# A map of row numbers that moves from a table of its own into the rows of x

## The reference

```python
x = layernorm(x + L0(x))     # two GIN convolutions and a linear layer
x = layernorm(x + L1(x))     # relational GCN, 8 edge types
x = layernorm(x + L2(x))     # GCN on the first 10000 nodes
x = layernorm(x + L3(x))     # three GAT layers

def gin_conv(x):             # in L0
    agg = segment_sum(x[src], dst, num_segments=50000)
    h = x + agg
    return relu(h @ wa + ba) @ wb + bb
```

## Time and profile before

| | |
|---|---|
| median of two runs | 3564.31 us (3557.01 to 3571.61) |
| span of the profiled execution | 5308.1 us |
| busy PE / DVE / ACT / POOL in it | 3134.5 / 2677.8 / 2356.1 / 2154.2 us |
| DMA packets, data | 430539, 673.46 MB |
| start block; dense part; gin1 | 0 to 49; 51 to 1465; 1465 to 1901 us |
| all other phases | 1901 to 5308 us |

### The profile page before, as it was taken

The page is one execution under the profiler, slowest core; times in us unless marked ns, Lnnn a source line. Parts: engine busy times, 40 slices in busy tenths (PEclk is TensorE's granted clock), DMA queues, the critical chain, the costliest instruction groups (busy, mean ns, idle before and its releaser), DMA issues. The chain is left out here.

```text
span 5308.1 us, 70155 instructions
## 1 busy us (share of the span) xinstructions
PE 3134.5 (59%) x18625; PEld 2527.0 (48%) x18625; DVE 2677.8 (50%) x8976; ACT 2356.1 (44%) x6177; POOL 2154.2 (41%) x2226
## 2 busy tenths in 40 slices
PE   1110107999867779868756403997029970178864
PEld 1000006777644445534446403996029870177764
DVE  1000008999943346559846301775006860199875
ACT  0000007999812224447735302775017750188765
POOL 6777760000045555546366473001740017500366
PEclk7555559999967777779967656987559975598555
DMA  2200004444434433425556423765227752276542
GB/s 77 56 9 8 18 9 140 174 172 170 164 117 127 119 87 108 112 90 168 164 155 200 142 63 104 225 196 163 62 72 233 220 177 61 58 245 232 169 125 82
DMA packets 430539, 673.46 MB, mean 127 GB/s; under 512 B 81411, under 2 KB 168086, under 8 KB 430252
## 3 DMA queue, kind: packets, MB, share of 16 engines
q1 hardware_dynamic: 354764, 558.83, 32.6%
q0 software_dynamic: 70464, 108.96, 8.9%
q10 hardware_dynamic: 5024, 2.30, 0.2%
HBM read 378.46 MB, written 295.50 MB: 127 GB/s over the span
## 5 line engine op out<-in xcount | busy, mean ns | idle before, releaser
L647 POOL DMA_INDIRECT msgs<-t_gat,row_i x600 | 574.3, 957 | 1081.6 <-POOLq L157 895.1
L664 POOL DMA_INDIRECT dg_g_ring<-in_x,dst_i x200 | 192.2, 961 | 860.5 <-DVE g_xb L1222 782.9
L2229 ACT ACTIVATE t_nnt<-t_p_nt,cxt 128x512 f32<-128x512 f32 x294 | 200.4, 682 | 756.0 <-remote 265.3
L1754 PE MATMUL t_p_q<-mean_col,t_nsq 128*128 128x1 f32 x2352 | 332.6, 263 | 273.2 <-issue 243.0
L1754 PEld LDWEIGHTS t_p_q<-mean_col,t_nsq 128*128 128x128 f32 x2352 | 342.9, 224 | 280.8 <-issue 280.8
L2023 POOL DMA_INDIRECT out_rows<-t_x,own_i x200 | 204.4, 1022 | 491.1 <-ACT t_x L2279 437.9
L2109 PE MATMUL t_p_nt<-ident,t_nh 128*128 128x128 f32 x1176 | 217.7, 316 | 309.3 <-issue 176.1
L1747 PE MATMUL t_p_nh<-wx,t_nnt 128*128 128x132 f32 x1568 | 265.1, 320 | 178.9 <-issue 156.1
L800 PE MATMUL de_p_o<-wc,de_hh 128*128 128x128 f32 x1568 | 225.8, 289 | 151.5 <-DVE de_r L948 124.3
L2109 PEld LDWEIGHTS t_p_nt<-ident,t_nh 128*128 128x128 f32 x1176 | 158.1, 163 | 328.9 <-issue 231.4
L1747 PEld LDWEIGHTS t_p_nh<-wx,t_nnt 128*128 128x128 f32 x1568 | 228.4, 221 | 179.9 <-issue 179.4
(11 more groups left out here) (405 smaller groups left out, 9434.7 us busy)
## 6 DMA issues: line engine op xcount, KB each, us to landing
t_nh<-t_gat SPq DMA_DIRECT2D x294, 264.0 KB
t_gat<-t_nhn SPq DMA_DIRECT2D x196, 264.0 KB
t_x<-de_x SPq DMA_DIRECT2D x196, 256.0 KB
t_ah<-t_gat SPq DMA_DIRECT2D x150, 264.0 KB
t_x<-t_x SPq DMA_DIRECT2D x148, 256.0 KB
t_gat<-t_ahn SPq DMA_DIRECT2D x100, 264.0 KB
t_gat<-de_h SPq DMA_DIRECT2D x98, 264.0 KB
de_x<-in_x SPq DMA_DIRECT2D x97, 256.0 KB
```

The source lines that it names most:

```text
L647: self.nc.gpsimd.indirect_dma_start(out=self.msgs[:, c, 0:width], out_offset=None, in_=table, in_offset=bass.IndirectOffsetOnAxis(ap=idx[: ...
L664: nc.gpsimd.indirect_dma_start(out=ring[:, u, j, :], out_offset=None, in_=a["x"], in_offset=bass.IndirectOffsetOnAxis(ap=self.dst_i[:, i * ...
L1754: last = self.nc.tensor.matmul(p_q[:, j:j + 1], sq[:, j * D:(j + 1) * D], self.mean_col[:], start=True, stop=True)
L2229: nc.scalar.activation(nnt[:, g % 2], p_nt[:], ACT.Identity, bias=bias).then_inc(act_nt, 1)
```

## The change

The map gets a place in the rows of x. A new table `t_xw` has rows of 129 floats: 128 of x and the row number as the 129th float. One indirect gather by `src` then brings x and the row number.

- The start block: ACT writes SLOTS + node into the 129th float of all 50176 rows, in seven DMAs of 4-byte elements, behind its loads. SP writes zeros into x's place in the rows N to NPAD, and the store of the old map goes. The `dst` list is loaded and turned first in place of `src`.
- The dense block: SP issues 16 DMAs that copy x, memory to memory, 3125 rows of 512 bytes each into rows 516 bytes apart, ahead of its first load of x.
- POOL: gathers x by `dst` into `msgs` (24 in the start block, 168 then, 8 later), waits for `map_filled` and scatters the slot numbers to every 129th float, waits for the copy and the scatters, and gathers rows of 129 floats by `src` into the ring. The 200 look-ups and the zeros into `msgs` go.
- gin1: `msgs` and the ring change places. DVE copies the 129th floats to `row_i` in every group, and ACT waits for DVE's sum of bias and `msgs` (`dve_b`) before it writes `hidden` over that part of `msgs`.
- Slots without an edge of their own (partition 0) gather the zero row N.

```diff
+MW = D + 1
+COPIES = 16
+FILLS = 7
+LATE = 8
...
-        self.where = dram("t_where", NPAD + SLOTS, 1, I32)
+        xw = nc.dram_tensor("t_xw", (NPAD * MW + SLOTS,), F32, kind="Internal").ap()
+        self.places = xw.rearrange("(r o) -> r o", o=1)
+        self.xw = xw[0:NPAD * MW].rearrange("(r w) -> r w", w=MW)
+        self.unplaced = xw[NPAD * MW:NPAD * MW + SLOTS].rearrange("(p c) -> p c", p=128)
...
                     act.dma_start(dst, src).then_inc(loaded, 16)
+                act.wait_ge(self.nodes_told, 1)
+                t = NPAD // 128
+                rows = self.xw[0:NPAD, D:MW].rearrange("(p t) o -> p (t o)", p=128)
+                for n in range(FILLS):
+                    part = slice(n * t // FILLS, (n + 1) * t // FILLS)
+                    act.dma_start(rows[:, part], self.node_row[:, part]).then_inc(self.map_filled, 16)
...
             sp.dma_start(self.t4[SLOTS:SLOTS + 128, :], spread[:, 3, :]).then_inc(stored, 16)
+            for n in range(N, NPAD, 128):
+                m = min(NPAD, n + 128)
+                sp.dma_start(self.xw[n:m, 0:D], spread[0:m - n, 3, :]).then_inc(stored, 16)
...
-    def slot_gathers(self, pool, ring, sem, arrived, turned, copied):
+    def slot_gathers(self, pool, ring, sem, arrived, turned, taken):
...
             for j in range(G4):
                 nc.gpsimd.indirect_dma_start(
-                    out=ring[:, u, j, :], out_offset=None, in_=a["x"],
-                    in_offset=bass.IndirectOffsetOnAxis(ap=self.dst_i[:, i * G4 + j:i * G4 + j + 1], axis=0)).then_inc(arrived[u], 16)
-
-        def look(c):
-            nc.gpsimd.indirect_dma_start(
-                out=self.row_i[:, c:c + 1], out_offset=None, in_=self.where,
-                in_offset=bass.IndirectOffsetOnAxis(ap=self.src_i[:, c:c + 1], axis=0)).then_inc(self.map_taken, 16)
-
-        self.resident_gather(self.src_i, a["x"], D, got, range(FIRST, CHUNKS))
+                    out=ring[:, u, j, :], out_offset=None, in_=self.xw,
+                    in_offset=bass.IndirectOffsetOnAxis(ap=self.src_i[:, i * G4 + j:i * G4 + j + 1], axis=0)).then_inc(arrived[u], 16)
+
+        self.resident_gather(self.dst_i, a["x"], D, self.got, range(FIRST, CHUNKS - LATE))
+        pool.wait_ge(self.map_filled, 16 * FILLS)
         for c in range(CHUNKS):
             nc.gpsimd.indirect_dma_start(
-                out=self.where, out_offset=bass.IndirectOffsetOnAxis(ap=self.put_i[:, c:c + 1], axis=0),
+                out=self.places, out_offset=bass.IndirectOffsetOnAxis(ap=self.put_i[:, c:c + 1], axis=0),
                 in_=self.slot_id[:, c:c + 1], in_offset=None).then_inc(mapped, 16)
-        for i in range(UN):
-            rows(i)
...
-        ahead = CHUNKS - (AG - UN)
-        for c in range(ahead):
-            look(c)
-        for i in range(UN, AG):
-            rows(i)
-            look(ahead + i - UN)
-        pool.wait_ge(self.map_taken, 16 * CHUNKS)
+        self.resident_gather(self.dst_i, a["x"], D, self.got, range(CHUNKS - LATE, CHUNKS))
+        pool.wait_ge(self.x_copied, 16 * COPIES)
+        pool.wait_ge(mapped, 16 * CHUNKS)
+        for i in range(AG):
+            rows(i)
...
                 sp.wait_ge(s["cleared"], 1)
+                for n in range(COPIES):
+                    part = slice(n * N // COPIES, (n + 1) * N // COPIES)
+                    sp.dma_start(self.xw[part, 0:D], a["x"][part, :]).then_inc(self.x_copied, 16)
...
                     if live(k, u, 4, AG):
                         act.wait_ge(s["pe_b"], i - 3)
+                        act.wait_ge(s["dve_b"], i - 3)
...
+                    if live(k, u, 1, AG):
+                        dve.wait_ge(arrived[v], 16 * G4 * (k + (0 if u < 1 else 1)))
+                        nc.vector.tensor_copy(self.row_i[:, bass.ds((i - 1) * G4, G4)], xs[:, v, :, D]).then_inc(s["dve_row"], 1)
```

More of the change, by code:

```diff
@@ L178, in allocate @@
         self.got = ctx.enter_context(nc.semaphore("got"))
+        self.x_copied = ctx.enter_context(nc.semaphore("x_copied"))
+        self.map_filled = ctx.enter_context(nc.semaphore("map_filled"))
         def sb(name, shape, dt=F32):
@@ L416, in turn @@
             last.then_inc(columns, 1)
-        return load, store, fill, fold, turn, stored, ready
+        return load, store, fill, fold, turn, ready
     def segments_parts(self, sb, ps, sem):
@@ L558, in find @@
             dve.wait_ge(turned, 1)
-            nc.vector.tensor_copy(both(self.dst_i[:]), of(1)).then_inc(v, 1)
+            nc.vector.tensor_copy(both(self.src_i[:]), of(0)).then_inc(v, 1)
             nc.vector.tensor_copy(both(self.own_i[:]), of(2)).then_inc(v, 1)
@@ L583, in turn @@
             idp = self.ident[0:ROWP, 0:ROWP]
-            for n in range(1, 6):
+            for n in (0, 2, 3, 4, 5):
                 for j in range(2):
@@ L604, in _ @@
                 w_store(sp)
-                g_store(sp, zeroes)
+                g_store(sp)
             @block.scalar
@@ L1041, in hidden, with gin1_part @@
         return t[:, bass.ds(g, 1), 0:GN].rearrange("p o f -> p (o f)")
-    def gin1_part(self, block, sem, xd, arrived, turned, copied):
+    def gin1_part(self, block, sem, xs, arrived, turned, taken):
         nc, a = self.nc, self.a
@@ L1244, in phase_dense_gin1 @@
         with ctx:
-            ring = sb("g_ring", [128, UN, G4, D])
+            ring = sb("g_ring", [128, UN, G4, MW])
             block = ctx.enter_context(nc.Block())
             arrived = [sem(f"g_arrived{u}") for u in range(UN)]
-            turned, copied = sem("g1_turned"), sem("g1_copied")
-            self.dense_part(block, lambda n: sem("de_" + n), lambda pool: self.slot_gathers(pool, ring, sem, arrived, turned, copied))
-            self.gin1_part(block, lambda n: sem("g1_" + n), ring, arrived, turned, copied)
+            turned, taken = sem("g1_turned"), sem("g1_taken")
+            self.dense_part(block, lambda n: sem("de_" + n), lambda pool: self.slot_gathers(pool, ring, sem, arrived, turned, taken))
+            self.gin1_part(block, lambda n: sem("g1_" + n), ring, arrived, turned, taken)
     def phase_gin2(self):
```

111 lines of the change are left out of this document (52 added, 59 removed).

## The result

The changed kernel takes 3855.09 us (median of two runs, 3842.92 to 3867.26), against 3564.31 us: a ratio of 1.0832, 95% interval 1.0777 to 1.0886. It is slower, by 291 us.

The account below looks back on a forecast made before the run. Before: dense block bound by DVE, then gin1 by POOL, ending at 1078 us. After: 390 us to the first dense group + 676 + 285 = 1351, so +273: 3564 + 273 = 3837 us, range 3670 to 4080.

Parts of the forecast that it names:

- The bound before: Timed kernel before: dense block bound by DVE, 6.9 us a group, 676 us; gin1 paced by POOL, ending at 1078 us.
- the stall: Before, 51 to 800 us of the profile: PE, DVE, ACT nearly idle beside POOL; 738 us, assumed absent from timed runs.
- 63 us before POOL: Kernel before without the stall: dense block ends at 727 us, 63 us ahead of POOL's readiness for the fifth ring group.
- (1) The look-ups: POOL and gin1: 200 transfers leave POOL, its work before gin1 falls to 490 us; gin1, paced by PE, takes 285 us.
- (2) The row numbers: Start block: 50176 single-float writes by ACT cost 80 to 230 us of queue time, delaying the block's end 15 us.
- rival D: Start block: row-number writes hold ACT, the block ends up to 140 us later, time 3962 us; chance 0.06.
- (3) The copy: Ahead of the dense block: 256 us on five engines, plus 42 for gathers and 26 for writes, 324 us in all.
- the 127-row load: Load at L1080 in the trace before: 127 rows of 512 B at 20 GB/s, one engine's worth; the copy's rate basis.
- B: Copy spreads over many engines and costs 210 us instead of 324: 3723 us, 3700 to 3760; chance 0.18.
- C: Copy: writes at a pitch of 516 B cost twice the read, 4067 us; chance 0.09.
- E: Stall of 749 us is partly in timed runs too, so the change is faster by 72 us; chance 0.07.
- F: Dense block: loads of x pass the copy, which runs beside it; no difference, about 3540 us; chance 0.10.

Follow-up runs that it names:

- E8: Changed kernel with the row numbers written in one transfer in place of seven: 3861.56 us, ratio 1.0831 to the kernel before.
- E6: Changed kernel with copy slices of different row counts, each waited for, plus two 3125-row slices into rows 576 B apart: 4066.79 us.
- E7: Changed kernel with copy slices of 3120 rows (the last 3200) in place of 3125: 3717.18 us, ratio 1.0433 to the kernel before.
- E4: Changed kernel with the row numbers in one transfer, in a set where the kernel before takes 5333.97 us: 5105.14 us, ratio 0.958.
- E5: Changed kernel with the copy in 98 pieces behind the loads of x and row numbers in one transfer: 3519.72 us, ratio 0.9892 to before.
- E12: Kernel before without an edit, run again for a profile: 3571.4 us beside 3574.68, profiled span 3569.6 us.

## Why the prediction was right, step by step

**The bound before.** That the timed runs didn't hold the stall was right for the set that gave the median, and the reason given, that the surplus adds up to the stalled stretches, was sound. Two sizes were off and nearly made up for each other. The dense part takes 737 us, not 676. Some 24 of these 61 us are its start and end, from the first transpose to the first sum and behind the last one, for which 98 steps have no term; the changed kernel, at 6.84 us a group, takes 700 us with them. The others come from the pace, which was read from 950 to 1350 us, where POOL was idle. Beside POOL's gathers and look-ups it held, at 6.95 us a group, but not beside the writes into the old map, at 7.94, which the forecast put at nothing. And "63 us before POOL" was wrong: POOL is ready for its fifth ring group at 763 us, 22 us ahead of the dense part's end. gin1 was POOL's from that group on, 6.3 us a group, forecast 6.25. Its end: 1111 against 1078 us.

**(1) The look-ups.** gin1 takes 267 us, forecast 285; PE's 5.3 us a group for the 5.7 taken. POOL's work ahead of the ring ends at 569 us; the forecast said 541, from a start block that ended 28 us sooner.

**(2) The row numbers.** Block's end at 79 us, forecast 66, from 51 and 43 for before in the two profiles. The price of a row number was right: they pass from 18 to some 95 us, 1.5 ns each, where the lower price was 1.6. But ACT is held 60 us, until about one of the seven transfers is left, not two or three. And that the row numbers still in the engines' way at the block's end would delay the copy, by 12 us, was not in the sum. This is rival D at a quarter of its size, and E8 shows that it can't be had back by freeing ACT alone.

**(3) The copy.** 349 us from the block's end to the first transpose; forecast 324. The loads of x are no term of their own in it: SP issues three of them from 404.2 us on, while the last rows of the copy still pass, and the first transpose starts 1 us after these. Five engines, by the 127-row load alone, is right: E6 has 3125 rows at 20.25 us, a fifth of the 103.4 us that 3127 rows take on one, and E7 takes the issues of the same copy down to 191 us. The terms beside it were not. The cost of a row was 32.7 ns, against the 25.6 that 20 GB/s gave: 50000 rows on five engines are 327 us, not 256 + 26. So the writes were mis-sized, 27% and not 10%, and most of it is not the pitch: the padded rows too took 28 to 31 ns. POOL's gathers were put at 42 us, because they take a fifth of every engine's time; 149 rows a us beside them and 152 beside its writes make that some 4 us. Packets' times don't add up on an engine: the row numbers from 20 to 75 us take 130.4% of 16 engines' time by themselves, so packets overlap there, and those of the copy and the gathers may do the same. 327, 4 and the 12 us of the row numbers are 343 of the 347 us from SP's first issue to the copy's last row. The mechanism was right, but that the sum came within 25 us is partly luck: the price of the rows was 45 us too low, the 12 us were missing, and the gathers' price was 38 us too high.

**The sum.** gin1's end 1397 us against 1351 forecast (+13 block, +25 copy, +24 dense, -18 gin1, and 2 between), before 1111 against 1078 (+33): the difference 286 for 273. The time, 3855.09 for 3837.

**The rivals.** B (many engines) is refuted by E6; as a kernel of its own, E7, it gives 3717.18 us, where B was put at 3723. C (rows 516 B apart at twice the price) is refuted by E6: 4 to 14%. D came at a quarter of its size, as said. E (the stall counts, faster) is right for the other kind of set: there the change in the form of E4 is 4.2% faster, with the dense part from 560 to 1288 us, forecast "from about 541 to 1217"; the changed kernel itself was not run there. Where before takes 3564 us, nothing of this rival is left: the dense part's 37 us lie beside POOL's writes into the old map and not beside its other transfers. F (the loads pass the copy) is refuted by SP's timeline; the half of it that says that the traffic fits beside the dense part is right, as E5 shows with 3519.72 us, where F was put at 3540.

## What to carry to other kernels

Cut a copy into numbers of rows that divide by 16, and read the DMA share of a load in the trace before you trust its rate. Don't queue a bulk copy ahead of the loads that everyone waits for: the same bytes cost 349 us in front and, in pieces behind the loads, at most 18 (a dense part of 718 us against 700). When a profile's span doesn't fit the timed runs, find the stretches that hold the surplus first, and run the kernel before in the same set as whatever it is compared with. And when a stage slows down beside another engine's work, take its pace by stretch: here one of three kinds of transfer did all the harm.

## What was not expected of the hardware

- One kernel without an edit takes 3563 to 3575 us in some sets of runs and 5284 to 5334 in others. In the second kind PE, DVE and ACT nearly stand while POOL issues indirect transfers without a break (DVE 35 us in 749), and run when POOL waits now and then (665 us in 862). Why, and what selects the kind, stays open.
- 50176 writes of 4 bytes take the 16 engines for over 70 us: 40219 of them passed from 20 to 75 us in the profile after, and 5672 behind 81 us. Issuing them in one transfer cost ACT 0.60 us (E8), in seven 60.00 us, so an issue seems to wait until earlier transfers have gone far enough; what is behind it on that engine waits too.
- A copy from memory to memory in rows of 512 B has a floor of 3.3 to 4.1 ns a row, reached with 9 engines or so (E6).
- POOL's 200 indirect writes of 4 bytes into a table without gaps slow the dense groups beside them from 6.95 to 7.94 us, because the loads of x come late; the same writes 516 B apart don't (E12, E5). Why is open.
